# Small expert tiles placed between big ones in a mixture-of-experts stage

## What is computed

```python
x = x + tanh(g_xattn[0]) * attention(layernorm(x), ctx, ctx)      # 16 heads
xt = layernorm(x).reshape(-1, D)
logits = xt @ Wr + br
top_vals, top_idx = top_k(logits, 2)
gate = softmax(where(mask, logits, -inf))
h = relu(einsum('td,edh->teh', xt, W1) + b1)
y = einsum('teh,ehd->ted', h, W2) + b2
x = x + tanh(g_ffn[0]) * einsum('ted,te->td', y, gate)
```

## Time and profile before

| | us |
|---|---|
| median of three runs | 851.81 (851.7 to 854.1) |
| the profiled execution | 851.28 |
| its span, first to last instruction | 849.5 |
| TensorE busy | 735.1 (87%) |
| VectorE busy | 608.1 (72%) |
| GpSimd busy | 458.1 (54%) |
| ScalarE busy | 407.2 (48%) |
| mean granted TensorE clock | 0.959 |

### The profile page before, as it was taken

One profiled execution on the slowest core, in us unless ns is written; L12 is line 12 of the kernel. 1 busy time (PEld: TensorE's weight loads), 2 busy tenths in 40 slices (PEclk: granted clock), 3 DMA queues, 4 the chain that ended last, 5 costly groups with the idle time before them and its releaser, 6 DMA issues.

```text
span 849.5 us, 21395 instructions
## 1 busy us (share of the span) xinstructions
PE 735.1 (87%) x6536; PEld 491.0 (58%) x6537; DVE 608.1 (72%) x1256; ACT 407.2 (48%) x783; POOL 458.1 (54%) x453
## 2 busy tenths in 40 slices
PE   3688989898988889876899898899999999999982
PEld 2345545454545545433667676577777777767761
DVE  4767898989898987984356874657666666666653
ACT  3266777776777766764323323233333333333340
POOL 5224545665666655547436665754555555566432
PEclk9899999999999998987889999999999999999997
DMA  5446656667776675552312322342232233222321
GB/s 176 126 130 188 186 162 196 154 168 170 183 182 180 174 182 137 169 150 52 101 20 33 49 47 32 46 55 42 45 49 46 47 49 49 49 44 50 45 32 20
DMA packets 96789, 85.32 MB, mean 100 GB/s; under 512 B 22256, under 2 KB 86000, under 8 KB 96592
## 3 DMA queue, kind: packets, MB, share of 16 engines
q1 hardware_dynamic: 80752, 65.73, 28.7%
q0 software_dynamic: 15680, 18.69, 13.9%
q10 hardware_dynamic: 288, 0.00, 0.0%
HBM read 53.61 MB, written 30.62 MB: 99 GB/s over the span
## 4 chain that ended last, share of the span: by engine, by line
PE 33%; DMA 20%; DVE 18%; issue 16%; POOL 6%; ACT 4%; POOLq 0%; DVEq 0%; ACTq 0%; SPq 0%
DMA out_dram<-yb,dest_idx 17%; PE banks L1767 7%; DVE negmax L1121 6%; PE banks L1663 4%; PE banks L1579 3%; PE banks L1749 3%; PE banks L1751 3%; PE banks L1750 3%; POOL xg L704 3%; ACT probs L933 2%; PE banks L1651 2%; POOL token_lists L689 2%; PE banks L1565 2%; PE banks L1630 2%; DVE stats L1045 2%
## 5 line engine op out<-in xcount | busy, mean ns | idle before, releaser
L996 ACT ACTIVATE hid<-banks,b_col 128x256 f32<-128x256 f32 (+1 forms) x312 | 124.2, 451 | 226.0 <-PE banks L1751 119.3
L1767 PE MATMUL banks<-wall,hh 128*128 x568 | 207.3, 384 | 1.3 <-DVE hl L1460 0.9
L780 POOL DMA_INDIRECT out_dram<-yb,dest_idx x71 | 122.6, 1727 | 146.1 <-DMA out_dram<-yb,dest_idx 85.8
L1121 DVE TENSOR_REDUCE negmax<-banks 128x4 f32<-128x1024 f32 x128 | 155.8, 1217 | 23.0 <-PE banks L1630 22.1
L1749 PE MATMUL banks<-xh,wall 128*128 128x256 f16 (+1 forms) x624 | 164.7, 268 | 5.3 <-ACT hid L996 4.3
L933 ACT ACTIVATE probs<-banks 128x1024 f32<-128x1024 f32 x128 | 131.0, 1024 | 71.7 <-PE banks L1651 69.4
L1750 PE MATMUL banks<-xl,wall 128*128 128x256 f16 (+1 forms) x624 | 164.5, 268 | 0.0
L1751 PE MATMUL banks<-xh,wall 128*128 128x256 f16 (+1 forms) x624 | 164.4, 268 | 0.0
L1767 PE MATMUL banks<-wall,hl 128*128 x568 | 145.7, 276 | 0.0
L1663 PE MATMUL banks<-probs,vaug 128*32 128x256 f32 x1024 | 84.6, 402 | 26.7 <-ACT probs L933 16.1
L689 POOL DMA_INDIRECT token_lists<-entry,place_i x64 | 69.3, 1082 | 68.3 <-ACT probs L933 44.0
(11 more groups left out here) (203 smaller groups left out, 1178.4 us busy)
## 6 DMA issues: line engine op xcount, KB each, us to landing
raw<-in_L_ffn_W SPq DMA_DIRECT2D x16, 512.0 KB, 5.5
wst<-in_L_ffn_W SPq DMA_DIRECT2D x16, 512.0 KB, 6.3
k_parts<-kparts SPq DMA_DIRECT2D x48, 128.0 KB, 5.3
q_parts<-qparts SPq DMA_DIRECT2D x48, 128.0 KB
ks<-k_parts SPq DMA_DIRECT2D x64, 96.0 KB, 2.3
qs<-q_parts SPq DMA_DIRECT2D x64, 96.0 KB, 2.2
xin<-in_x SPq DMA_DIRECT2D x16, 256.0 KB, 2.9
cin<-in_ctx SPq DMA_DIRECT2D x16, 256.0 KB, 3.3
```

What stands on the lines that cost most here:

```text
L780: nc.gpsimd.indirect_dma_start(out_rows, bass.IndirectOffsetOnAxis(dest_idx[par][:, s:s + 1], 0), yb[par][:, s, :], None, compute_op=ALU.a ...
L996: ins = nc.scalar.activation(hid[half][:, c % (HC // 2), 0:subs(j) * P], banks[:, b, c % 2 * TS:c % 2 * TS + subs(j) * P], ACT.Relu, bias= ...
L1121: nc.vector.tensor_reduce(negmax[:, c, 8 * (g // 2):8 * (g // 2) + 8].rearrange("p (m g p2) -> p m g p2", m=2, g=2)[:, :, g % 2, :], banks ...
L1767: ins = nc.tensor.matmul(dst, h_[:, c, s * P:(s + 1) * P], w_, start=(c == 0 and k == 0), stop=(c == HC - 1 and k == 1))
```

## The change

The tiles get a new order: 25 big ones, then small and big ones in turn from tile 25 on, 25 small, 26 big, ... 37 small, 38 big. The tables in memory keep their order, all big entries first; `entry_of` maps a tile to its entry, `slot_at`, `subs_to` and `smalls_to` count sub-tiles in the new order. The small tiles lose what was theirs alone: `gather_small`, the semaphores xg_half, `half_of`, `y_bank` and `after_small`. They go through the same buffers, banks and instruction order as big ones, with one sub-tile in place of two. The transposes stand at chunk 2 where first's tile is small, else at chunk 4 as before. The loop ends with step 21 in place of step 29; the rest is fixed code. The slot loads from tile 25 on wait for the table of small tiles. The value loads in the step functions of all engines take entry_of in their fixed steps.

```diff
@@ -377,7 +376,7 @@
...
-            laps = BIGS // 2 - 1
+            laps = (MIXED - 2) // 2
@@ -394,25 +393,28 @@
...
+        MIXED = NT - 2 * SMALLS
+        assert MIXED % 2 == 1 and TILE_LEAD < MIXED - 3
+
+        def smalls_to(j):
+
+            return max(0, j - MIXED + 1) // 2 if isinstance(j, int) else 0
+
         def subs(j):
 
-            return SUB if not isinstance(j, int) or j < BIGS else 1
+            return 1 if isinstance(j, int) and j >= MIXED and (j - MIXED) % 2 == 0 else SUB
...
-            return SUB * j if not isinstance(j, int) or j <= BIGS else SUB * BIGS + j - BIGS
-
-        def subs_to(lap):
-
-            return SUB * lap if not isinstance(lap, int) or lap <= BIGS // 2 else SUB * BIGS // 2 + lap - BIGS // 2
-
-        def half_of(j):
-
-            return (j - BIGS) // 2 % 2
-
-        def y_bank(j, par, s):
-
-            return 6 + (s if subs(j) == SUB else par)
+            return SUB * j - smalls_to(j)
+
+        def subs_to(lap, par):
+
+            return SUB * lap - (smalls_to(2 * lap) if isinstance(lap, int) and par else 0)
+
+        def entry_of(j):
+
+            return j if subs(j) == SUB and smalls_to(j) == 0 else j - smalls_to(j) if subs(j) == SUB else BIGS + smalls_to(j)
@@ -593,14 +595,14 @@
...
-            for j in range(EARLY, BIGS):
+            for j in range(EARLY, MIXED):
                 slot_load(j)
             hold(sp, table_ready, 6)
-            for j in range(BIGS, NT):
+            for j in range(MIXED, NT):
                 slot_load(j)
 
-            hold(sp, y_sent[0], 16 * subs_to((NT + 1) // 2))
-            hold(sp, y_sent[1], 16 * subs_to(NT // 2))
+            hold(sp, y_sent[0], 16 * subs_to((NT + 1) // 2, 0))
+            hold(sp, y_sent[1], 16 * subs_to(NT // 2, 1))
@@ -695,7 +697,7 @@
...
-                wait(pool, xg_full[par], 16 * subs_to(lap))
+                wait(pool, xg_full[par], 16 * subs_to(lap, par))
@@ -703,20 +705,6 @@
...
-
-            def gather_small(j, par):
-                h, turn = half_of(j), (j - BIGS) // 4
-                if turn == 0:
-                    hold(pool, xg_full[par], 16 * SUB * (BIGS // 2))
-                    hold(pool, gT_done, BIGS - 1 + par)
-                else:
-                    hold(pool, xg_half[par][h], 16 * turn)
-                    hold(pool, gT_done, j - 3)
-                hold(pool, slots_full[par], 16 * (j // 2 + 1))
-                nc.gpsimd.tensor_copy(gather_idx[par][:, h:h + 1].unsqueeze(2), slots[:, slot_at(j):slot_at(j) + 1, 0:1]).then_inc(idx_ready, 1)
-                hold(pool, idx_ready, j + 1)
-                nc.gpsimd.indirect_dma_start(xg[par][:, h, :], None, xn2_d,
-                                             bass.IndirectOffsetOnAxis(gather_idx[par][:, h:h + 1], 0)).then_inc(xg_half[par][h], 16)
@@ -774,9 +762,9 @@
...
-                    wait(pool, y_sent[1 - par], 16 * subs_to(lap + par))
+                    wait(pool, y_sent[1 - par], 16 * subs_to(lap + par, 1 - par))
                 else:
-                    hold(pool, y_sent[par], 16 * (subs_to(lap) + 1))
+                    hold(pool, y_sent[par], 16 * (subs_to(lap, par) + 1))
@@ -788,13 +776,8 @@
...
-                if not fixed or 2 <= j < BIGS - 2:
+                if there(j, 2) and not (fixed and j < 2):
                     gather(j + 2, t + 1, i)
-                elif j >= BIGS - 2:
-                    ahead = (2 * j - BIGS + 4, 2 * j - BIGS + 5) if j < BIGS else (j + 4,)
-                    for x_ in ahead:
-                        if x_ < NT:
-                            gather_small(x_, x_ % 2)
@@ -1500,25 +1483,23 @@
...
-                    wait(dve, y_sent[par], 16 * subs_to(lap))
+                    wait(dve, y_sent[par], 16 * subs_to(lap, par))
...
-                link(nc.vector.scalar_tensor_tensor(out=yb[par][:, s, :], in0=banks[:, y_bank(j, par, s), 0:D], scalar=1.0 / HSCALE / WSCALE,
+                link(nc.vector.scalar_tensor_tensor(out=yb[par][:, s, :], in0=banks[:, 6 + s, 0:D], scalar=1.0 / HSCALE / WSCALE,
                                                     in1=b2_b[:, ds(e, 1), :].rearrange("p e d -> p (e d)"), op0=ALU.mult, op1=ALU.add))
-                link(nc.vector.scalar_tensor_tensor(out=yb[par][:, s, :], in0=banks[:, y_bank(j, par, s), D:2 * D], scalar=1.0 / HSCALE / WSCALE,
+                link(nc.vector.scalar_tensor_tensor(out=yb[par][:, s, :], in0=banks[:, 6 + s, D:2 * D], scalar=1.0 / HSCALE / WSCALE,
...
-                after_small = fixed and j > BIGS
                 if there(j, -1):
-                    e = dve.value_load(tile_expert[0:1, ds(j - 1, 1)], min_val=0, max_val=E - 1)
-                if there(j, -1) and not after_small:
+                    e = dve.value_load(tile_expert[0:1, ds(entry_of(j - 1) if fixed else j - 1, 1)], min_val=0, max_val=E - 1)
@@ -1537,8 +1518,6 @@
...
-                    if half == 0 and after_small and there(j, -1):
-                        result(j - 1, (j - 1) // 2, 1 - i, 0, e)
@@ -1724,15 +1703,11 @@
...
-                if subs(j) == SUB:
-                    pe.wait_ge(xg_full[par], 16 * subs_to(lap + 1))
-                else:
-                    pe.wait_ge(xg_half[par][half_of(j)], 16 * ((j - BIGS) // 4 + 1))
+                pe.wait_ge(xg_full[par], 16 * subs_to(lap + 1, par))
                 wait(pe, xl_ready, j - 1)
                 for s in range(subs(j)):
-                    src = xg[par][:, s if subs(j) == SUB else half_of(j), :]
                     for m in range(M):
-                        ins = nc.tensor.transpose(banks[:, 4 + par, m * TS + s * P:m * TS + (s + 1) * P], src[:, m * P:(m + 1) * P], ident[:])
+                        ins = nc.tensor.transpose(banks[:, 4 + par, m * TS + s * P:m * TS + (s + 1) * P], xg[par][:, s, m * P:(m + 1) * P], ident[:])
@@ -1756,13 +1731,9 @@
...
-                    if subs(j) == SUB:
-                        wait(pe, y_ready, slot_at(j - 1) + s + 1)
-                    else:
-                        pe.wait_ge(y_ready, slot_at(j - 2) + 1 if j - 2 >= BIGS else slot_at(BIGS - 1) + 1 + par)
+                    wait(pe, y_ready, slot_at(j - 1) + (s + 1 if s < subs(j - 1 if isinstance(j, int) else j) else 0))
                 both = wall[:, ds(e, 1), 1, 0:2, c * D:(c + 1) * D].rearrange("p e s n -> p (e s) n")
-                at = y_bank(j, par, s)
-                mm = [(banks[:, at, 0:2 * D], hh[par], both), (banks[:, at, 0:D], hl[par], both[:, 0, :])]
+                mm = [(banks[:, 6 + s, 0:2 * D], hh[par], both), (banks[:, 6 + s, 0:D], hl[par], both[:, 0, :])]
@@ -1861,9 +1832,9 @@
...
-                    e1 = pe.value_load(tile_expert[0:1, ds(j + 1, 1)], min_val=0, max_val=E - 1)
+                    e1 = pe.value_load(tile_expert[0:1, ds(entry_of(j + 1) if isinstance(j, int) else j + 1, 1)], min_val=0, max_val=E - 1)
                 if there(j, -1):
-                    e2 = pe.value_load(tile_expert[0:1, ds(j - 1, 1)], min_val=0, max_val=E - 1)
+                    e2 = pe.value_load(tile_expert[0:1, ds(entry_of(j - 1) if isinstance(j, int) else j - 1, 1)], min_val=0, max_val=E - 1)
@@ -1878,7 +1849,7 @@
...
-                    if there(j, 2) and c == HC // 2:
+                    if there(j, 2) and c == (HC // 2 if not isinstance(j, int) or subs(j + 1) == SUB else 2):
```

More of the change, by code:

```diff
@@ L313, in flamingo @@
         xg_full = [sem(f"xg_full{i}") for i in range(2)]
-        xg_half = [[sem(f"xg_half{i}{h}") for h in range(2)] for i in range(2)]
         gT_done, xh_ready, xl_ready = sem("gT_done"), sem("xh_ready"), sem("xl_ready")
@@ L526, in slot_load @@
                 wait(sp, slots_full[j % 2], 16 * (j // 2))
-                base = sp.value_load(tile_base[0:1, j:j + 1], min_val=0, max_val=LISTED - subs(j) * P)
+                base = sp.value_load(tile_base[0:1, entry_of(j):entry_of(j) + 1], min_val=0, max_val=LISTED - subs(j) * P)
                 sp.dma_start(slots[:, slot_at(j):slot_at(j + 1), :],
@@ L1001, in step @@
                 if there(j, 1):
-                    e = act.value_load(tile_expert[0:1, ds(j + 1, 1)], min_val=0, max_val=E - 1)
+                    e = act.value_load(tile_expert[0:1, ds(entry_of(j + 1) if isinstance(j, int) else j + 1, 1)], min_val=0, max_val=E - 1)
                     for b in range(2):
```

## The result

The changed kernel takes 877.64 us (median of four, 875.48 to 879.24) against 852.95 us before on the same chips: 1.028 of the time, 95% interval 1.0239 to 1.0322. It is slower by 24.7 us. The profiled execution reported 879.24 us at a span of 877.4, 28.0 us more than the one of before (851.28). Medians are of all runs; the ratios leave out two runs whose granted clock was low throughout, one of the kernel before in the series of e1 to e4 (967.2 us, clock 0.737) and one of e7 (1074.33 us, clock 0.643).

A forecast was written before the change was run, and what follows sets the result against it. TensorE, busy 87%, was taken to bound the kernel, with gaps only in the small run. Waits, tail and loop summed to +23.2 us and the clock to +11.9, on 851.3: 886 us, range 862 to 897.

The forecast's parts named there:

- rival A: Both waits of the small steps come, at xl and at gathered rows, but the clock stays up: 874 us, chance 0.25.
- Part 1: VectorE runs a small tile's result before the next big tile's low_x: TensorE waits 2.8 us, six times, 16.8 us.
- Part 2: Big tiles' gathers queue behind a scatter: TensorE waits 1.85 us at small steps' transposes, six times, 11.1 us.
- Part 3: After step 37: 4.7 us idle before second(38); span ends 12.65 us after the last matmul, 1.15 us won.
- Part 4: Loop of 4 laps instead of 8 wins at most 0.9 us; slot loads, index arithmetic and semaphores change nothing.
- Part 5: Idle of 2.8 us drops TensorE's clock: 1.7 us on each of six big steps and second(38), 11.9 us.
- granted clock below 0.9: Sign expected in the profile after, from step 25 on, that TensorE's clock had dropped.
- The reading ahead of the sum: TensorE has no gap in steps whose tiles are all big, 10.88 us each; only the small run has gaps.
- B: Gathers arrive in time and only VectorE's order costs: 863 us, chance 0.08.
- C: Longer waits, 3.2 us for gathered rows, and the clock down after both: 894 us, to 897, chance 0.10.
- D: Faster: the small run's 8.3 us of latency vanish and the hand-over is no wait: 845 us, chance 0.07.
- E: Hand-overs to the big step come to about 0.8 us, so no change: 851 us, chance 0.04.

The follow-up runs named there:

- e1: The changed kernel with VectorE's low_x for the next big tile put ahead of the small tile's result: 869.52 us, ratio 1.022.
- e4: The changed kernel with the transposes of small steps moved back from chunk 2 to chunk 4: 875.71 us, ratio 1.0307.
- e7: e5 with the tile order moved by one, so that the last tile is small: 860.06 us, ratio 1.0072.
- e3: The changed kernel with only GpSimd's order changed, big tiles' gathers issued one step earlier: 871.72 us, ratio 1.0213.
- e9: e5 with all gathers from step 22 on issued one step earlier, small tiles' too: 848.75 us, ratio 0.9961.
- e6: The changed kernel with idle matmuls put where TensorE waits, results unchanged: 876.8 us, ratio 1.0308.
- e12: The kernel before, its tile order kept, with only the big tiles' gathers issued one step earlier: 842.2 us, ratio 0.9873.
- e8: e5 with TensorE's two value loads of a fixed step moved from its head to chunk 4 of the step before: 869.79 us, ratio 1.0203.
- e5: e2 and e3 together on the changed kernel: 858.23 us, ratio 1.0079.
- e2: e1 with second's two banks used in turn by sub-tile number: 860.09 us, ratio 1.0092.

## Why the prediction was right, step by step

The forecast of 886 us was 8.4 us above the median and 6.8 above the profiled execution; the range of 862 to 897 holds both. By the number alone the median is nearer to rival A (874, 3.6 us away) than to the forecast. It is the trace that decides between them: the clock did fall, which A denies.

- **Part 1 (VectorE's order).** Right to the place, the count and nearly the size: six waits, 2.53 us as the profile draws them, 2.7 us from the end of the step's work to L1724, against 2.8. e1 confirms the cause: with the order alone undone the waits are gone.
- **Part 2 (the gather behind the scatter).** Right in place and cause (e3, e9). Seven waits of 10.3 us in sum against 12.0: the scatter came later than counted, since the clock stretched the big step's first half, but the landings were quicker in four cases of the six (2.8 to 3.1 us from the second gather's issue, as from 764.41 to 767.20, against 3.75 from 786.04 to 789.79). I had put 3.6 for all. The first scatter of a big step stood 7.6 us behind its start where the clock was up (730.59 to 738.16), against the 7.5 counted, and 8.9 to 9.1 where it was down. Of the six waits, 0.86 to 2.79 us, only two lie in the 1.5 to 2 us that were to show it.
- **Part 3 (the tail).** 4.3 us of idle against 4.7, and 12.2 us from the last matmul's end to the span's end (865.15 to 877.4) against 12.65.
- **Part 4 (the rest).** 0.9 us were put on the shorter loop. Tile 25 came 1.5 us earlier, but 1.15 us of that stand at tile 13 already (563.01 against 564.16), ahead of the loop in both kernels, so the loop didn't make them. Between tiles 25 and 31 the kernel before lost 0.8 us to the loop's drift and the 1.63 us of the earlier trace rows (696.35 to 764.05 are 67.7 us, six steps of 10.88 are 65.3). The drift is saved, and the 1.63 us, which I left standing, didn't come back. Together that is 3.9 us instead of 0.9, 3.0 us of the miss.
- **Part 5 (the clock).** Right in direction and in price, too high in count: seven falls were put down, five came (four hand-overs of six, and before the last tile). Five pairs from 724.10 to 833.54 take 109.44 us; take off 5 x 16.3 of work, 5 x 2.7 for xl and the gather waits of 6.5, and 8 us are left. By pair it is 0.4 behind the first hand-over, which kept its clock, then 1.8 to 2.0. So a fall costs 1.4 to 1.6 us here, 1.6 to 1.9 in e4's pairs, and second(38) took 7.6 us (857.54 to 865.15) against 5.4 in e9 (831.55 to 836.92). That makes some 8 us where 11.9 were put, the largest single miss. The sign "granted clock below 0.9" didn't show either: it was 0.94 from 730 to 840. e1, e4 and e6 tie it to the 2.5 us of idle: taken away or filled, the clock is 1.00; with only the gather waits taken away it stays at 0.94. Rival A (clock up, 874) falls by that. Why the clock held at two hand-overs of six wasn't found.
- **The miss, added up.** Of the 7.1 us between 35.1 and 28.0, part 1 has 0.6, part 2 has 1.7, part 3 has 0.4 + 0.4, part 4 has 3.0 and part 5 has 3.8. Some 0.4 us in each of six pairs, which the sum didn't have and which stand in the pair without a fall too, go the other way. So it is 7.5 us by this count: errors of one sign in most terms, not one wrong step.
- **The reading ahead of the sum**, that the big steps have no gap, was too broad. It holds from 564.16 on but for 0.2 us at 641.47 and the 1.63 us at 764.05; between 430 and 570 us TensorE waited 10.2 us for gathered rows in big steps, as part 5 itself says. The sum isn't touched by it, but e12 shows that more was to be won there than in the order of the tiles.
- **The rivals.** B (gathers in time) and C (longer waits) have no trace. D and E, the cases without a loss, needed a hand-over below 0.8 us; it took 2.7 + 1.5. But D came near as to what the order would be worth if it were so: 845.6 expected, and e9, which has neither wait but 2.6 us of idle before the last tile, measured 848.75.
- **A claim beside the sum**, that chunk 2 gains nothing where rows are late: e4 agrees in the waits, and in the stage of its profile (8 us less); in the median it isn't resolved.

## What to carry to other kernels

When short units are put between long ones in a software pipeline, go through each in-order engine and ask what stands in front of the operation that opens the next step. A result that came mid-step for a long unit comes at the very end for a short one, and everything queued behind it becomes late. Issue a prefetch ahead of the operations that wait for results, not behind them: here, issuing the gathers one step earlier, ahead of one step's scatters, was worth 9.8 us to the kernel before, more than the order of the tiles.

## What the runs showed of the hardware

- Where two value loads on TensorE's queue stood behind a gather wait, TensorE sat idle for 0.8 to 1.0 us more before its next matmul (e8, five times). In the changed kernel's family idle stands at the head of each big step behind a small one (0.74 to 0.92 us in e1, 0.16 to 0.66 in e5, 0.22 to 0.32 in e9, where the head comes without a late rows wait before it). Since e8 moved the loads away from e5's heads and their idle went, it is the loads' in e5; in e1 and e9 that is likely and not shown.
- The length of an idle stretch alone didn't decide on the clock. It fell to 1.2 GHz at four of six waits of 2.53 us in the changed kernel and not at the other two. It fell after 1.96 us (e8, 806.26) and 1.95 us (the changed kernel, 513.21, fall at 513.8), and stayed up after 2.79 us (the changed kernel, 724.10) and 2.80 us (e2, 729.23), and in e1, where waits of 2.1, 0.85 and 0.4 us stood within one and a half steps. In e8, 1.2 to 1.4 us followed by 0.95 to 0.99 us dropped it three times. What decides wasn't found.
- A fall cost 1.4 to 1.9 us of a step each time (the changed kernel and e4).
- The landing of a gather of 128 rows varied between 2.8 and 3.8 us behind its issue in the same place of the same step. What chooses between the two wasn't tried.
